# Expert mixture: weights loaded and split two experts at a time, mostly inside a written-out first unit

## The chip, the core and the metric

The program runs on one core of one Trainium2 chip. The core has TensorE (PE: matmuls into PSUM banks), VectorE (DVE), ScalarE (ACT), GpSimd (POOL) and SyncE (SP), which here only issues transfers (DMA) between the chip's memory and the on-chip SBUF. Each engine runs its own instructions in order and meets the others at semaphores. The metric is the device time of one execution in microseconds (us); lower is better.

## What is computed

The program is a graph network of two layers; the change concerns one stage of it, the feed-forward part of layer 0. Its input is the sum of two row sets in memory (`x1`, the linear-attention output, and `hidden`, the graph attention output), 6250 rows of 256. On each normalised row eight experts work, each with three 256x256 weights, and a softmax router weighs them:

```python
BN_EPS = 0.001
def _bn(h, g, b, m, v):
    return g * (h - m) * jax.lax.rsqrt(v + BN_EPS) + b
w = jax.nn.softmax(feat @ Wr + br, axis=-1)
h = jnp.einsum('bfd,edh->bfeh', x, W1) + b1
h = jax.nn.relu(_bn(h, g1, be1, m1, v1))
h = jnp.einsum('bfeh,ehk->bfek', h, W2) + b2
h = jax.nn.relu(_bn(h, g2, be2, m2, v2))
y = jnp.einsum('bfeh,ehd->bfed', h, Wo) + bo
return jnp.einsum('bfed,fe->bfd', y, w)
```

Here E (e) is 8 experts, D and H are 256, and `x` is the sum of the rows, normalised, with a leading axis of one; the result is added to that sum.

## The kernel before

`build` runs the stages one after the other; `expert_mixture` (L3023) is one stage, inside a block of its own: none of its instructions starts before the stage ahead has ended, and the next stage starts when it is done.

**Units.** The 50 tiles of 128 rows are taken four at a time (`QUAD`): 13 units, the last of two tiles. Loaded rows lie in `x` and `h` (two slots each, both in the tile `moe_xh`). A unit adds them (`front_start`), takes the statistics of the rows (`front_statistics`), a square root on ACT (`front_root`), normalises (`front_end`, into `xn`), turns the rows with PE (`turn`) and copies them to `xt` on ACT (`turned`). The router's products (L3343, `moe_route`) need `xt`.

**Split products.** Matmuls are done in three passes on split numbers: a number is its rounded high part (type fp32r) plus the low part, and a product is high*high + high*low + low*high (`product`, L3327). So every weight, `xt` (`cut_rows`) and both hidden activations (`cut_layer`) are split: `high_part` (L3090) rounds, `low_part` (L3093) subtracts.

**Steps of a unit.** `unit` goes through steps e = 0 to 9. In step e PE does the first layer of expert e (`moe_first`), the second of expert e-1 (`moe_second`) and the third of expert e-2 (`moe_third`). ACT follows the first two with the batch norm and relu (`layer`, L3285, into `h12`, tile `moe_h`); DVE splits what ACT wrote and adds the third layer's result to `x` (`gather_expert`, L3213). In steps 2, 3 and 5 DVE also prepares the next unit's rows.

**Before the first unit.** SP loads 13 small tensors (router weights, biases and batch norm parameters, L3101), then W1 into the place of `h12` and W2 into that of `xh`, 2 MB each for all eight experts. PE turns the parameters (L3314) and DVE and ACT work out scale and shift (`gain`, `shift`) of the batch norms. DVE then rounds and splits W1 and W2, 4096 elements in each of 128 partitions at a time. Wo is loaded over W1 once W1 has been split, and the rows of the first two units over W2 once that has been split. PE waits for `s_cutw` 3, all three weights split, before its loop over six pairs of units; unit 13 is written out behind the loop.

Of the kernel before, what the change touches and what calls it, by code (L numbers as in the profile page):

```python
# [10 lines left out]
ALU = mybir.AluOpType  # L11
# [3 lines left out]
P = 128  # L15
# [3007 lines left out]
def expert_mixture(nc, io, dram, keep):  # L3023
# [11 lines left out]
    with ExitStack() as stack:  # L3035
        space = Space(nc, stack, "moe")
        sb, sem = space.sb, space.sem
        h12 = sb("h12", [P, 2, 2, HALVES, QUAD * P])
        w = [h12[:, :, :, :, :].rearrange("p j k a n -> p (j k a n)").rearrange("p (e a d) -> p e a d", e=E, a=HALVES)]
        w_high, w_low = ([sb(f"w_{n}{j}", [P, E, HALVES, D], F32R) for j in range(3)] for n in ("high", "low"))  # L3040
# [8 lines left out]
        x, h = xh[:, 0], xh[:, 1]  # L3049
        w.append(xh[:, :, :, :, :].rearrange("p j k i d -> p (j k i d)").rearrange("p (e a d) -> p e a d", e=E, a=HALVES))  # L3050
        xn = sb("xn", [P, QUAD, D])
# [15 lines left out]
        s_x, s_sent = space.sems("s_x", 2), space.sems("s_sent", 2)  # L3067
        s_wj = space.sems("s_wj", 3)
        s_and1, s_and2, s_cut1, s_cut2, s_andx, s_cutx, s_andw, s_cutw = (
            sem(n) for n in ("s_and1", "s_and2", "s_cut1", "s_cut2", "s_andx", "s_cutx", "s_andw", "s_cutw"))  # L3070
        (s_w, s_free, s_dve, s_std_in, s_std, s_xn, s_xt, s_xtc, s_l1, s_h1, s_l2, s_h2, s_l3, s_acc, s_route, s_logit, s_exp, s_gate,
# [5 lines left out]
        hidden = pair_rows(dram["hidden"])  # L3077
        w_loads = [(w[j % 2], io[f"L0_ffn_{n}"].rearrange("e (a p) n -> p e a n", p=P)) for j, n in enumerate(("W1", "W2", "Wo"))]
        loads = [(wr[:, :, :], io["L0_ffn_Wr"].rearrange("(a p) e -> p a e", p=P)), (br[:, :], rows_of(io["L0_ffn_br"])),
# [12 lines left out]
        def low_part(out, whole, high):  # L3092
            return nc.vector.tensor_tensor(out, whole, high.bitcast(F32), ALU.subtract)  # L3093

        with nc.Block() as block:

            @block.sync
            def _(sp):
                with nc.allow_non_contiguous_dma(reason="small routing weights"):
                    for to, frm in loads:  # L3100
                        sp.dma_start(to, frm).then_inc(s_w, 16)  # L3101
                for j, (to, frm) in enumerate(w_loads):
                    if j == 2:
                        sp.wait_ge(s_cutw, 1)
                    sp.dma_start(to, frm).then_inc(s_wj[j], 16)
                sp.wait_ge(s_cutw, 2)
                for s in range(2):
                    load(sp, s, slice(s * QUAD, (s + 1) * QUAD))

# [17 lines left out]
            def _(dve):  # L3127
                c = Count(dve, s_dve)

                for j in range(2):  # L3130
                    dve.wait_ge(s_par, j + 1)
                    last = nc.vector.tensor_copy(par[:, j], bank1[j][:, 0:5 * 16].rearrange("p (i e) -> p i e", i=5))
                c.done(last)
                c.done(nc.vector.memset(bn_eps[:, :], EPS))
                dve.sem_inc(s_var, 1)
                dve.wait_ge(s_root, 1)
                c.done(nc.vector.reciprocal(gain[:, :, :], shift[:, :, :]))
                c.done(nc.vector.tensor_tensor(gain[:, :, :], gain[:, :, :], par[:, :, 1, :], ALU.mult))
                c.done(nc.vector.tensor_tensor(shift[:, :, :], par[:, :, 0, :], par[:, :, 3, :], ALU.subtract))
                c.done(nc.vector.tensor_tensor(shift[:, :, :], shift[:, :, :], gain[:, :, :], ALU.mult))  # L3140
                nc.vector.tensor_tensor(shift[:, :, :], shift[:, :, :], par[:, :, 2, :], ALU.add).then_inc(s_scale, 1)
                dve.wait_ge(s_w, 16 * len(loads))

# [75 lines left out]

                def unit(n, s, m, next_loaded, size=QUAD):  # L3220

                    gates(n, s, size)
                    for e in range(E + 2):
# [16 lines left out]
                        if e == 5 and next_loaded is not None:  # L3240
                            front_end(n + 1, 1 - s)

                dve.sem_inc(s_acc, 1)
                for j in range(3):
                    dve.wait_ge(s_wj[j], 16)
                    high_part(w_high[j][:, :, :, :], w[j % 2]).then_inc(s_andw, 1)
                    dve.wait_ge(s_andw, j + 1)
                    low_part(w_low[j][:, :, :, :], w[j % 2], w_high[j][:, :, :, :]).then_inc(s_cutw, 1)
                    if j == 1:
                        front_start(0, 32)  # L3250
                        front_statistics(0)
                        front_end(1, 0)
                cut_rows(1)
                STEPS = 8
                with dve.Fori(0, N_U // 2) as r:
                    c.enter(r, 2 * STEPS)
                    for s in range(2):
                        unit(r * 2 + s + 1, s, r * (2 * E) + s * E, r * 32 + (32 if s == 0 else 64))
                c.leave(N_U // 2)
                unit(N_U, 0, (N_U - 1) * E, None, REST)  # L3260

            @block.scalar
            def _(act):
                act.wait_ge(s_var, 1)
                nc.scalar.activation(shift[:, :, :], par[:, :, 4, :], ACT.Sqrt, bias=bn_eps[:, 0:1]).then_inc(s_root, 1)
                act.wait_ge(s_scale, 1)
                act.sem_inc(s_h1, 1)
                act.sem_inc(s_h2, 1)

                def front_root(n):  # L3270
# [17 lines left out]

                def unit(n, s, m, last, size=QUAD):
                    act.wait_ge(s_logit, n)  # L3290
                    nc.scalar.activation(gate[:, s, 0:size], logit[:, 0:size, :], ACT.Exp).then_inc(s_exp, 1)
                    for e in range(E + 1):
                        if e < E:
                            layer(0, m + (e + 1), e, size)
                        if e == E and not last:
                            turned(n + 1)
                        if e >= 1:
                            layer(1, m + e, e - 1, size)
                        if e == 4 and not last:
                            front_root(n + 1)  # L3300

                front_root(1)
                turned(1)
                with act.Fori(0, N_U // 2) as r:
                    for s in range(2):
                        unit(r * 2 + s + 1, s, r * (2 * E) + s * E, False)
                unit(N_U, 0, (N_U - 1) * E, True, REST)

            @block.tensor
            def _(pe):  # L3310
                pe.wait_ge(s_w, 16 * len(loads))
                for j in range(2):
                    for i in range(5):
                        last = nc.tensor.transpose(bank1[j][:, 16 * i:16 * i + 16], par_rows[:, j, i, :], keep["ident"][0:16, 0:16])  # L3314
                    last.then_inc(s_par, 1)
                pe.wait_ge(s_scale, 1)

                def turn(n, s):
# [18 lines left out]

                def unit(n, s, m, last_unit, size=QUAD):

# [6 lines left out]
                    for e in range(E + 2):  # L3346
                        if e < E:

                            if e == 0:
                                pe.wait_ge(s_cutx, n)  # L3350
                            pe.wait_ge(s_h1, m + (e + 1))
                            wide(bank1, 0, e, (xt_high, xt_low), size).then_inc(s_l1, 1)
                        if e == 1:
# [4 lines left out]
                        if 1 <= e <= E:  # L3358
                            pe.wait_ge(s_cut1, m + e)
                            pe.wait_ge(s_h2, m + e)  # L3360
                            wide(bank2, 1, e - 1, (h1_high[:, (e - 1) % 2], h1_low[:, (e - 1) % 2]), size).then_inc(s_l2, 1)
                        if e == 2:
# [6 lines left out]
                        if e >= 2:  # L3369
                            pe.wait_ge(s_cut2, m + (e - 1))  # L3370
                            pe.wait_ge(s_acc, m + (e - 1))
                            for i in range(size):
# [6 lines left out]
                pe.wait_ge(s_cutw, 3)  # L3379
                with pe.Fori(0, N_U // 2) as r:  # L3380
                    for s in range(2):
                        unit(r * 2 + s + 1, s, r * (2 * E) + s * E, False)
                unit(N_U, 0, (N_U - 1) * E, True, REST)


# [502 lines left out]
```

## Time and profile before

| | us |
|---|---|
| median of 3 runs (7068.94 to 7074.64) | 7070.54 |
| the profiled execution, its own time | 7087.27 |
| its span, first to last instruction | 7085.5 |
| PE / DVE / ACT / POOL busy in it | 5313.8 / 4842.8 / 4142.8 / 3639.1 |

The profiled execution is 16.7 us above the median; 1.8 us of its own time lie outside the span. Times within the trace are us from the span's start. The expert mixture stage lies from about 4270 to 5301, a seventh of the span. Since the stages follow one another, a stage's time is that of its own longest chain, and the busy shares of the whole span say little about it.

### The profile page before, as it was taken

The numbers are of one execution on the slowest core, as the hardware profiler recorded it, in microseconds if no ns is written. First come the engines' busy times: TensorE is split into PE (matmuls) and PEld (weight loads), VectorE is DVE, ScalarE is ACT, GpSimd is POOL, SyncE is SP. The second block draws the span as 40 slices with busy tenths as digits, with TensorE's granted clock in tenths as the row PEclk, the third lists the DMA queues.
The fourth block names the chain that finished last, engine by engine and source line by source line (L and its number), as shares of the span: only waits on it lengthen the run. The fifth ranks groups of instructions, "written<-read, shape, count | busy, mean of one in ns | idle before, by whom it ended". The sixth has DMA issues, their size and how long they took to land. (4 is left out here: it accounts for less than half of the span.)

```text
span 7085.5 us, 94548 instructions
## 1 busy us (share of the span) xinstructions
PE 5313.8 (75%) x22314; PEld 3799.3 (54%) x22314; DVE 4842.8 (68%) x13222; ACT 4142.8 (58%) x13411; POOL 3639.1 (51%) x3571
## 2 busy tenths in 40 slices
PE   1768888745888886668888616999989787877688
PEld 1645555333555554545555315888874566655346
DVE  5656666694777777767777596666662677778673
ACT  4578888874898988579889762333336322111132
POOL 3477777737777773577777700000000577777201
PEclk8878888876999998779999767999999898887789
DMA  6444444344444443444444332000007534333302
GB/s 184 124 123 116 117 118 117 106 132 139 119 121 122 121 118 104 131 138 124 118 122 118 109 108 65 19 18 27 19 23 267 166 116 128 109 107 101 105 17 74
DMA packets 484001, 763.77 MB, mean 108 GB/s; under 512 B 85543, under 2 KB 360695, under 8 KB 483511
## 3 DMA queue, kind: packets, MB, share of 16 engines
q0 software_dynamic: 166320, 446.82, 22.7%
q1 hardware_dynamic: 317335, 313.36, 13.9%
q14 instruction: 253, 2.07, 0.1%
q8 instruction: 93, 1.52, 0.1%
HBM read 622.82 MB, written 146.27 MB: 109 GB/s over the span
## 5 line engine op out<-in xcount | busy, mean ns | idle before, releaser
L1806 POOL DMA_INDIRECT gm_got<-scratch_feat,keep_src_tab x2490 | 2500.6, 1004 | 776.0 <-issue 669.6
L2028 ACT ACTIVATE gm_got<-gm_got 128x64 f32<-128x64 f32 x9828 | 2393.6, 335 | 5.8 <-DVE gm_got L1941 5.8
L2083 PE MATMUL gm_bank<-gm_got,gm_onehot 128*128 128x264 f32 x4980 | 1783.1, 466 | 385.9 <-DVE gat_acc L1966 229.4
L2083 PEld LDWEIGHTS gm_bank<-gm_got,gm_onehot 128*128 128x128 f32 x4980 | 938.4, 217 | 897.8 <-DVE gat_acc L1966 370.1
L1966 DVE TENSOR_TENSOR gat_acc<-gat_acc,gm_bank 128x264 f32 x2490 | 1059.1, 425 | 498.8 <-PE gm_bank L2083 231.5
L1114 POOL DMA_INDIRECT mix1a_got<-scratch_rel_feat,layer_rel_tab x240 | 240.4, 1002 | 1529.2 <-issue 1528.0
L1114 POOL DMA_INDIRECT mix1b_got<-scratch_rel_feat,layer_rel_tab x590 | 586.9, 995 | 190.5 <-issue 187.2
L1171 PE MATMUL mix1b_m_bank<-mix1b_got,mix1b_onehot 128*128 128x256 f32 x1180 | 379.6, 459 | 153.6 <-DVE layer_acc L1145 132.1
L837 POOL DMA_INDIRECT scratch_first<-gat_scores,keep_first_pos x150 | 216.5, 1444 | 466.9 <-DVE gat_scores L820 425.7
L1973 DVE TENSOR_TENSOR gm_onehot<-keep_iota_row,keep_dst_tab 128x896 f32<-128x896 f32 x357 | 386.5, 1083 | 25.8 <-PE gm_bank L2083 21.9
L1171 PEld LDWEIGHTS mix1b_m_bank<-mix1b_got,mix1b_onehot 128*128 128x128 f32 x1180 | 245.7, 225 | 253.3 <-DVE mix1b_onehot L1123 166.4
L3285 ACT ACTIVATE moe_h<-moe_first,moe_shift,moe_gain 128x512 f32<-128x512 f32 (+1 forms) x208 | 147.1, 759 | 350.0 <-PE moe_first L3327 350.0
L3327 PE MATMUL moe_third<-moe_w_high,moe_cuts 128*128 128x256 f32 x1600 | 315.5, 290 | 29.5 <-DVE moe_xh L3213 29.5
L1145 DVE TENSOR_TENSOR layer_acc<-layer_acc,mix1b_m_bank 128x256 f32 x590 | 242.8, 412 | 86.3 <-PE mix1b_m_bank L1171 71.9
L3327 PEld LDWEIGHTS moe_third<-moe_w_high,moe_cuts 128*128 128x128 f32 x1600 | 262.7, 196 | 38.5 <-issue 34.8
L3090 DVE CAST moe_cuts<-moe_h 128x1024 fp32r<-128x1024 f32 (+1 forms) x208 | 140.1, 674 | 198.6 <-ACT moe_h L3285 196.7
L3093 DVE TENSOR_TENSOR moe_cuts<-moe_h,moe_cuts 128x1024 fp32r<-128x1024 f32 (+1 forms) x208 | 246.4, 1185 | 7.1
L3327 PE MATMUL moe_second<-moe_cuts,moe_w_high 128*128 128x512 f32 (+1 forms) x832 | 249.9, 383 | 0.0
L3767 POOL TENSOR_TENSOR slo_x<-slo_x,slo_b_out 128x512 f32<-128x512 f32 x25 | 31.0, 1269 | 419.3 <-DMA slo_x<-scratch_x 419.3
L3285 ACT ACTIVATE moe_h<-moe_second,moe_shift,moe_gain 128x512 f32<-128x512 f32 (+1 forms) x208 | 147.3, 759 | 166.4 <-PE moe_second L3327 166.4
L1665 PE MATMUL gm_side<-gm_w,gm_fft 128*128 128x256 f32 x800 | 244.0, 387 | 0.0
L505 ACT ACTIVATE mix1b_ln_std<-mix1b_ln_mv,keep_eps 128x2 f32<-128x2 f32 x75 | 16.8, 286 | 381.2 <-DVE mix1b_ln_mv L500 381.2
(558 smaller groups left out, 10760.2 us busy)
## 6 DMA issues: line engine op xcount, KB each, us to landing
scratch_rel_feat<-rel_out SPq DMA_DIRECT2D x50, 1024.0 KB, 6.3
gm_got<-scratch_feat,keep_src_tab POOLq DMA_INDIRECT x2490, 2.8
gm_flags<-scratch_flags SPq DMA_DIRECT2D x90, 280.0 KB
gf_feat<-scratch_feat SPq DMA_DIRECT2D x75, 256.0 KB, 4.4
gf_old<-scratch_hidden SPq DMA_DIRECT2D x75, 256.0 KB, 4.7
scratch_hidden<-gf_h SPq DMA_DIRECT2D x75, 256.0 KB, 4.0
scratch_feat<-gf_row SPq DMA_DIRECT2D x50, 260.0 KB, 3.3
gm_x<-scratch_x SPq DMA_DIRECT2D x50, 256.0 KB, 3.1
```

The lines of the kernel that those rows point to most:

```text
L1114: nc.gpsimd.indirect_dma_start(out=self.got[:, u, :], out_offset=None, in_=self.table, in_offset=bass.IndirectOffsetOnAxis(ap=self.keep["r ...
L1145: nc.vector.tensor_tensor(rows, rows, self.bank[p % self.BANKS][:, i * D:(i + 1) * D], ALU.add).then_inc(self.s_acc, 1)
L1171: last = self.nc.tensor.matmul(self.bank[p % self.BANKS][:, i * D:(i + 1) * D], self.onehot[:, u, :], self.got[:, u, :], start=True, stop= ...
L1665: nc.tensor.matmul(out, self.fft[:, c, i * P:(i + 1) * P], self.w2[:, c, :], start=(c == 0), stop=False)
L1806: nc.gpsimd.indirect_dma_start(out=got[:, place // GROUPS, place % GROUPS * GROUP + j, 0:GAT_ROW], out_offset=None, in_=dram["feat"][layer ...
L1966: nc.vector.tensor_tensor(a, a, bank[j % BANKS][:, 0:GAT_SUM], ALU.add).then_inc(s_acc, 1)
L1973: nc.vector.tensor_tensor(onehot[:, half:half + GROUP, :], keep["iota_row"][:, :].unsqueeze(1).to_broadcast([P, GROUP, P]), keep["dst_tab" ...
L2028: last = nc.scalar.activation(rows, rows, ACT.Copy, scale=got[:, b, i, D + h:D + h + 1])
L2083: nc.tensor.matmul(bank[i % BANKS][:, 0:GAT_SUM], onehot[:, i % HOTS, :], got[:, v[1] % B, i, :], start=True, stop=True).then_inc(s_sum, 1)
L3093: return nc.vector.tensor_tensor(out, whole, high.bitcast(F32), ALU.subtract)
L3285: last = nc.scalar.activation((h1, h2)[j][:, e % 2, a, 0:size * P], (bank1, bank2)[j][a][:, 0:size * P], ACT.Relu, bias=shift[:, j, q:q + ...
L3327: last = nc.tensor.matmul(out, lhs(k)[i], rhs(k)[j], start=(p == 0), stop=(p == len(passes) - 1))
```

## The change

The weights are loaded and split in four groups of two experts (`AT_ONCE = 2`, 512 KB for each weight) rather than all eight at once. High parts of weights are made by ACT, low parts by DVE. Only group 0 is done ahead of the first unit. That unit is written out before the loop, and groups 1 to 3 are done within it: group g of W1 after step 2g-2, of W2 and Wo after step 2g-1 (`group_due`). The whole weights pass through places not yet used: parts of `h12` for group 0, row slot 1 for W2 and Wo of group 1, and a new tile `spare` of two places in turn for the rest. The rows of the first unit are loaded ahead of everything, those of the second once group 1 of W2 and Wo has been split. The parameters are worked out after the first unit's rows. The loop runs over five pairs of units, starting with unit 2; unit 12 is written out behind it, then unit 13 as before.

```diff
             def _(sp):
+                load(sp, 0, slice(0, QUAD))
+                for j in range(3):
+                    load_weight(j, 0)
                 with nc.allow_non_contiguous_dma(reason="small routing weights"):
                     for to, frm in loads:
                         sp.dma_start(to, frm).then_inc(s_w, 16)
-                for j, (to, frm) in enumerate(w_loads):
-                    if j == 2:
-                        sp.wait_ge(s_cutw, 1)
-                    sp.dma_start(to, frm).then_inc(s_wj[j], 16)
-                sp.wait_ge(s_cutw, 2)
-                for s in range(2):
-                    load(sp, s, slice(s * QUAD, (s + 1) * QUAD))
+                for j in range(3):
+                    load_weight(j, 1)
+                load_weight(0, 2)
+                load_weight(1, 2)
+                for j in (1, 2):
+                    sp.wait_ge(s_cutw[j], 2)
+                load(sp, 1, slice(QUAD, 2 * QUAD))
+                load_weight(2, 2)
+                for j in range(3):
+                    load_weight(j, 3)
...
+                def load_weight(j, g):
+                    if (j, g) in SPARE[2:]:
+                        before_j, before_g = SPARE[SPARE.index((j, g)) - 2]
+                        sp.wait_ge(s_cutw[before_j], before_g + 1)
+                    sp.dma_start(whole(j, g), weights[j][:, experts(g), :, :]).then_inc(s_wg[j][g], 16)
...
+                def cut_weights(j, g):
+
+                    dve.wait_ge(s_high[j], g + 1)
+                    low_part(w_low[j][:, experts(g), :, :], whole(j, g), w_high[j][:, experts(g), :, :]).then_inc(s_cutw[j], 1)
...
+                def high_weights(j, g):
+                    act.wait_ge(s_wg[j][g], 16)
+                    nc.scalar.copy(w_high[j][:, experts(g), :, :], whole(j, g)).then_inc(s_high[j], 1)
...
+        def group_due(e):
+
+            if e % 2 == 0:
+                return [(0, e // AT_ONCE + 1)] if e // AT_ONCE + 1 < W_GROUPS else []
+            return [(j, (e + 1) // AT_ONCE) for j in (1, 2)] if (e + 1) // AT_ONCE < W_GROUPS else []
```

On PE the first unit's passes wait for their group: `s_cutw[0]`, `[1]` and `[2]` at e // 2 + 1 of the expert in hand. PE now turns the first rows, then the parameters, and waits for scale and shift (`s_scale`) before the router's products.

Ahead of the first unit, DVE's order before (tiles: `moe_par`, `moe_gain`, `moe_shift` are the parameters, `moe_h` and `moe_xh` the weights in their loading places, `moe_xn` the normalised rows):

```order
L3132 COPY moe_par<-moe_first 128x80 x2
...
L3141 TENSOR_TENSOR moe_shift<-moe_shift,moe_par 128x32
L3090 CAST moe_w_high<-moe_h 128x4096
L3093 TENSOR_TENSOR moe_w_low<-moe_h,moe_w_high 128x4096
L3090 CAST moe_w_high<-moe_xh 128x4096
L3093 TENSOR_TENSOR moe_w_low<-moe_xh,moe_w_high 128x4096
L3147 TENSOR_TENSOR moe_xh<-moe_xh 128x1024
...
L3164 TENSOR_SCALAR moe_xn<-moe_xh,moe_mv,moe_std 128x256 x4
L3090 CAST moe_w_high<-moe_h 128x4096
L3093 TENSOR_TENSOR moe_w_low<-moe_h,moe_w_high 128x4096
L3090 CAST moe_xt_high<-moe_xt 128x1024
L3093 TENSOR_TENSOR moe_xt_low<-moe_xt,moe_xt_high 128x1024
```

Here the parameters stand first and the rows between the second weight and the third. DVE's order of the change at the same place (router work, `moe_logit`, begins the unit):

```order
L3189 TENSOR_TENSOR moe_xh<-moe_xh 128x1024
...
L3206 TENSOR_SCALAR moe_xn<-moe_xh,moe_mv,moe_std 128x256 x4
L3096 TENSOR_TENSOR moe_w_low<-moe_h,moe_w_high 128x1024
L3093 CAST moe_xt_high<-moe_xt 128x1024
L3096 TENSOR_TENSOR moe_xt_low<-moe_xt,moe_xt_high 128x1024
L3169 COPY moe_par<-moe_first 128x80 x2
...
L3178 TENSOR_TENSOR moe_shift<-moe_shift,moe_par 128x32
L3096 TENSOR_TENSOR moe_w_low<-moe_h,moe_w_high 128x1024 x2
L3229 TENSOR_TENSOR moe_logit<-moe_route,moe_br 128x32
```

Three roundings and three subtractions of 4096 elements have become three subtractions of 1024, the rows stand first and the parameters behind them.

Within the first unit, DVE's order of the change in steps 2 and 3 (the `moe_w_low` rows are added; the rest stood in the loop's body in the same order):

```order
L3255 SCALAR_TENSOR_TENSOR moe_xh<-moe_third,moe_gate,moe_xh 128x256 x4
L3189 TENSOR_TENSOR moe_xh<-moe_xh 128x1024
L3096 TENSOR_TENSOR moe_w_low<-moe_spare,moe_w_high 128x1024
L3093 CAST moe_cuts<-moe_h 128x1024
L3096 TENSOR_TENSOR moe_cuts<-moe_h,moe_cuts 128x1024
L3093 CAST moe_cuts<-moe_h 128x1024
L3096 TENSOR_TENSOR moe_cuts<-moe_h,moe_cuts 128x1024
L3255 SCALAR_TENSOR_TENSOR moe_xh<-moe_third,moe_gate,moe_xh 128x256 x4
L3194 BN_STATS moe_stats<-moe_xh 128x6 x4
L3198 BN_AGGR moe_mv<-moe_stats 128x2 x4
L3096 TENSOR_TENSOR moe_w_low<-moe_spare,moe_w_high 128x1024 x2
L3093 CAST moe_cuts<-moe_h 128x1024
```

A subtraction now stands behind the next unit's first sum in step 2, and two behind its statistics in step 3. On ACT the roundings stand at the end of the same steps:

```order
L3332 ACTIVATE moe_h<-moe_second,moe_shift,moe_gain 128x512 x2
L3315 CAST moe_w_high<-moe_spare 128x1024
L3332 ACTIVATE moe_h<-moe_first,moe_shift,moe_gain 128x512 x2
L3332 ACTIVATE moe_h<-moe_second,moe_shift,moe_gain 128x512 x2
L3315 CAST moe_w_high<-moe_spare 128x1024 x2
```

In the loop's body of before, ACT has only the two `moe_h` rows in each step; the one rounding (step 2) and the two (step 3) stand between them.

## Rows read from the trace of the kernel before

**Rows 1.** Timeline, SP and PE: start us, us, engine, line, (idle before <-releaser).

```profile
4270.39 0.38 SPq L3101 DMA_DIRECT2D moe_wr<-in_L_ffn_Wr  x1
...
4276.09 0.41 SPq L3101 DMA_DIRECT2D moe_par_rows<-in_L_ffn_v  x1
...
4277.01 2.00 SPq L3105 DMA_DIRECT2D moe_xh<-in_L_ffn_W  x1
4277.71 1.24 PE L3314 MATMUL moe_first<-keep_ident,moe_par_rows 16*128 16x16 f32 x10 [162.10 <-DMA moe_par_rows<-in_L_ffn_v]
```

**Rows 2.** Timeline, the parameters on DVE, first and last.

```profile
4278.45 0.24 DVE L3132 COPY moe_par<-moe_first 128x80 f32<-128x80 f32 x1 [11.49 <-PE moe_first L3314]
...
4280.86 0.19 DVE L3141 TENSOR_TENSOR moe_shift<-moe_shift,moe_par 128x32 f32<-128x32 f32 x1
```

**Rows 3.** Timeline, weights and rows ahead of the first unit.

```profile
4284.82 2.29 DVE L3090 CAST moe_w_high<-moe_h 128x4096 fp32r<-128x4096 f32 x1 [3.77 <-DMA moe_h<-in_L_ffn_W]
4287.15 4.43 DVE L3093 TENSOR_TENSOR moe_w_low<-moe_h,moe_w_high 128x4096 fp32r<-128x4096 f32 x1
...
4298.26 0.37 SPq L3085 DMA_DIRECT2D moe_xh<-scratch_x  x1
...
4303.83 1.23 DVE L3147 TENSOR_TENSOR moe_xh<-moe_xh 128x1024 f32<-128x1024 f32 x1 [5.60 <-DMA moe_xh<-scratch_hidden]
```

**Rows 4.** Timeline, from normalised rows to PE's first product.

```profile
4307.60 1.38 DVE L3164 TENSOR_SCALAR moe_xn<-moe_xh,moe_mv,moe_std 128x256 f32<-128x256 f32 x4
...
4309.13 1.09 PE L538 MATMUL moe_turn<-keep_ident,moe_xn 128*128 128x128 f32 x4 [30.18 <-DVE moe_xn L3164]
...
4311.59 0.59 ACT L3277 COPY moe_xt<-moe_route 128x512 f32<-128x512 f32 x1
...
4315.56 0.69 DVE L3090 CAST moe_xt_high<-moe_xt 128x1024 fp32r<-128x1024 f32 x1
...
4315.89 3.57 PE L3343 MATMUL moe_route<-moe_wr,moe_xt 128*128 128x8 f32 x16 [4.82 <-DVE moe_w_low L3093]
...
4319.31 0.77 PE L3327 MATMUL moe_first<-moe_xt_high,moe_w_high 128*128 128x512 f32 x1
```

**Rows 5.** Groups of ACT by form: a copy of 1024 elements.

```profile
L3775 ACT COPY slo_lhs<-ffn_slice_t 128x1024 f32 x25 | 25.7, 1045 | 63.4 <-PE slo_bank L3786 53.9 <-PEq L3779 9.5
```

**Rows 6.** DVE line L3093 alone: min/median/max ns of one, at 1024 elements.

```profile
L3093 DVE TENSOR_TENSOR moe_xt_low<-moe_xt,moe_xt_high x13: 1225/1226/1227, 4316.3 to 5246.1; 128x1024 fp32r<-128x1024 f32 x13
```

**Rows 7.** Timeline of unit 1, steps 3 and 4, PE, ACT and DVE.

```profile
4345.26 0.62 PE L3327 MATMUL moe_second<-moe_cuts,moe_w_high 128*128 128x512 f32 x2
...
4345.46 1.45 ACT L3285 ACTIVATE moe_h<-moe_first,moe_shift,moe_gain 128x512 f32<-128x512 f32 x2 [6.29 <-PE moe_first L3327]
...
4346.94 0.70 DVE L3090 CAST moe_cuts<-moe_h 128x1024 fp32r<-128x1024 f32 x1 [1.10 <-ACT moe_h L3285]
...
4351.53 1.65 DVE L3213 SCALAR_TENSOR_TENSOR moe_xh<-moe_third,moe_gate,moe_xh 128x256 f32<-128x256 f32 x4
...
4353.22 1.40 DVE L3152 BATCH_NORM_STATS2 moe_stats<-moe_xh 128x6 f32<-128x256 f32 x4
...
4353.60 0.62 PE L3327 MATMUL moe_second<-moe_cuts,moe_w_high 128*128 128x512 f32 x2
...
4355.28 0.69 DVE L3090 CAST moe_cuts<-moe_h 128x1024 fp32r<-128x1024 f32 x1
...
4356.32 0.28 PE L3327 MATMUL moe_third<-moe_w_high,moe_cuts 128*128 128x256 f32 x1
```

**Rows 8.** Windows: length; PE, PEld, DVE, ACT, POOL busy; PEclk, DMA, GB/s.

```profile
4280.00:4290.00 10.00, 0.00 (x0) 0.00 (x0) 6.06 (x7) 0.00 (x0) 0.00 (x0) 0.50 1.08 350
```

**Rows 9.** Timeline, PE's router products behind the loop's turns.

```profile
4474.75 1.95 PE L3343 MATMUL moe_route<-moe_wr,moe_xt 128*128 128x8 f32 x16 [0.71 <-issue]
...
4941.83 3.58 PE L3343 MATMUL moe_route<-moe_wr,moe_xt 128*128 128x8 f32 x16 [2.52 <-issue]
```

**Rows 10.** DMA issues of the stage: KB each, us to landing.

```profile
moe_xh<-scratch_hidden SPq DMA_DIRECT2D x10, 512.0 KB, 5.0
```

More of the change, by code:

```diff
@@ L3241, in unit @@
                             front_end(n + 1, 1 - s)
+                        if cutting:
+                            for j, g in group_due(e):
+                                cut_weights(j, g)
                 dve.sem_inc(s_acc, 1)
[L3244 to L3252, printed above, removed]
+                front_start(0, 32)
+                front_statistics(0)
+                front_end(1, 0)
+                cut_weights(0, 0)
                 cut_rows(1)
+                parameters()
+                for j in (1, 2):
+                    cut_weights(j, 0)
                 STEPS = 8
-                with dve.Fori(0, N_U // 2) as r:
+                unit(1, 0, 0, 32, cutting=True)
+                with dve.Fori(0, N_U // 2 - 1) as r:
                     c.enter(r, 2 * STEPS)
-                    for s in range(2):
-                        unit(r * 2 + s + 1, s, r * (2 * E) + s * E, r * 32 + (32 if s == 0 else 64))
-                c.leave(N_U // 2)
+                    for s in (1, 0):
+                        k = 2 - s
+                        unit(r * 2 + k + 1, s, r * (2 * E) + k * E, r * 32 + 64)
+                c.leave(N_U // 2 - 1)
+                unit(N_U - 1, 1, (N_U - 2) * E, 32 * (N_U // 2 + 1))
                 unit(N_U, 0, (N_U - 1) * E, None, REST)
@@ L3287, in layer, with unit @@
                     last.then_inc((s_h1, s_h2)[j], 1)
-                def unit(n, s, m, last, size=QUAD):
+                def unit(n, s, m, last, size=QUAD, cutting=False):
                     act.wait_ge(s_logit, n)
@@ L3297, in unit @@
                         if e >= 1:
+                            if cutting and e == 2:
+                                act.wait_ge(s_cutw[2], 1)
                             layer(1, m + e, e - 1, size)
@@ L3378, in _ @@
                 turn(1, 0)
[L3379 to L3382, printed above, removed]
+                pe.wait_ge(s_w, 16 * len(loads))
+                for j in range(2):
+                    for i in range(5):
+                        last = nc.tensor.transpose(bank1[j][:, 16 * i:16 * i + 16], par_rows[:, j, i, :], keep["ident"][0:16, 0:16])
+                    last.then_inc(s_par, 1)
+                pe.wait_ge(s_scale, 1)
+                unit(1, 0, 0, False, cutting=True)
+                with pe.Fori(0, N_U // 2 - 1) as r:
+                    for s in (1, 0):
+                        k = 2 - s
+                        unit(r * 2 + k + 1, s, r * (2 * E) + k * E, False)
+                unit(N_U - 1, 1, (N_U - 2) * E, False)
                 unit(N_U, 0, (N_U - 1) * E, True, REST)
```

90 lines of the change are left out of this document (57 added, 33 removed).

## Prediction

> **What bounds the kernel now.** The page comes first: no engine is busy for more than three quarters of the span, and the stages follow one another, so the question is what the chain of this one stage is. The timeline of its start answers it. SP issues the first small load at 4270.39, PE has the parameters at 4277.71 [rows 1], and then DVE alone works: each weight costs it 2.29 us of rounding and 4.43 us of subtraction [rows 3], 6.7 us, or 20.2 us for the three, with a wait of 3.77 us for W1 ahead of them. The rows of unit 1 can be loaded only when W2's place is free, so SP issues them at 4298.26 [rows 3]. The wait that ends last ahead of the unit is PE's for `moe_w_low`, at 4315.89; its first layer product starts at 4319.31, 48.92 us after the stage's first load [rows 4]. Behind that, in unit 1 as in the others, PE is the bound: one step takes 8.34 us (4345.26 to 4353.60, the same pass of the next expert) and PE has no gap in it [rows 7], while DVE has holes of about a microsecond. So what the stage takes ahead of 4319.31 counts in full, and work on ACT and DVE in unit 1 counts only where it makes PE wait.
>
> **The new chain ahead of unit 1, step by step.** All from 4270.39, where the rows' load now stands.
> (a) From issue to DVE's sum of the two row sets: 4298.26 to 4303.83 [rows 3], 5.57 us, to 4275.96.
> (b) Sum, statistics, square root and normalising: 4303.83 to the end of `moe_xn`, 4308.98 [rows 3, 4], 5.15 us, to 4281.11.
> (c) PE's turn and ACT's two copies: 4308.98 to 4312.18 [rows 4], 3.20 us, to 4284.31.
> (d) Splitting `xt`: 4315.56 to the end of the subtraction, 0.69 us and 1.23 us with 0.03 us between them [rows 4, 6], 1.95 us, to 4286.26.
> (e) The parameters, now behind that: 4278.45 to 4281.05 [rows 2], 2.60 us, to 4288.86.
> (f) The router's products: 4315.89 to 4319.31 [rows 4], 3.42 us, to 4292.28.
> The first product starts at 4292.28 rather than at 4319.31: 27.03 us earlier.
>
> What is taken to cost nothing, and what hides it. The three weight loads of group 0 stand behind the rows. At 350 GB/s, the rate of the stretch in which the 2 MB loads run [rows 8], 512 KB take 1.5 us, so they land at 4277.5, 4279.0 and 4280.5. ACT rounds 1024 elements in about 1.05 us, by a copy of that width [rows 5]: W1 to 4278.5, before its square root is wanted (4279.2), W2 and Wo behind its `xt` copies, 4284.3 to 4286.4, before the parameters' square root (about 4287). DVE's subtraction of W1 (1.23 us [rows 6]) fills its wait for the turn. Those of W2 and Wo, 2.45 us from 4288.86, end at 4291.3, within the router's products. The 13 small loads are issued from 4272.8 to about 4278.5, 0.48 us apart (twelve distances from 4270.39 to 4276.09) and, with 1.6 us from the last issue to use [rows 1], are there at 4280.5 to 4281; PE turns them after 4283.2, 1.24 us [rows 1], while DVE still splits. PE comes out of its long wait at a granted clock of 0.50, 1.2 GHz [rows 8]; (c) and (f) are read behind that wait, and in the changed kernel they again follow one, so I change nothing for the clock.
>
> Here a rule of the Trainium skill speaks against the change. The trace first: the thirteen small loads of [rows 1] overlap, and the last lands 1.6 us behind its issue; so DMAs in one queue do not pay their latency one after another. The page "DMA: Bandwidth & Descriptors" (section Bandwidth) says to batch transfers to 1 MiB or more, since each costs some 2.0 us fixed plus its bytes at 436 GB/s. Paid in series, five loads of 512 KB would by that page take 16 us and the 13 small ones another 26, the stage would start no earlier than now, and the change would be worth nothing.
>
> **Unit 1 with the rest of the weights.** It holds nine roundings of 1.05 us on ACT (9.4 us) and nine subtractions of 1.23 us on DVE (11.0 us) [rows 5, 6]. ACT has two activations of 1.45 us [rows 7] in a step of 8.34 us and has room. DVE is the one to count. The fullest place is behind step 3's statistics: DVE runs without a wait from its addition at 4351.53 over the statistics at 4353.22 to its next rounding at 4355.28 [rows 7], and two subtractions more, 2.45 us, move that to 4357.73. It enters step 3 hardly late, since the one subtraction of step 2 (1.23 us) falls into a hole of 1.10 us [rows 7] and what is left is absorbed by the next. From 4357.73 it has two splits (1.95 us each) and the addition (1.65 us) to do: 4363.28. PE wants the addition for its third layer at 4356.32 + 8.34 = 4364.66 [rows 7]. The margin is 1.4 us; the split itself is wanted at 4353.60 + 8.34 = 4361.94 and is there at 4359.7. Steps 4 and 5 have as much. Bounds: nothing if the margin holds; if it fails, at most the subtractions that stand beyond one per step, three of 1.23 us, 3.7 us. Below nothing it can't go, as no work leaves unit 1. I take 0.5 us, near the row.
>
> **Loads inside unit 1.** SP now holds the second unit's rows until `s_cutw[1]` and `[2]` are 2, DVE's end of step 1, some 19 us behind the first product; queued behind this wait are one 512 KB load of Wo and three of group 3. The rows land 5.6 us later by (a), 5.0 by the loads inside the stage [rows 10], and DVE wants them at the end of step 2, more than 6 us later. Each other late load has a whole step of 8.34 us against 5.0 [rows 10]. I take nothing.
>
> **The written-out unit.** PE's router products wait for "issue" 0.71 and 2.52 us behind turns of the loop [rows 9] (a third wait there is shorter). The change trades one turn for the loop's entry between units 1 and 2. Between -2.5 and 2.5 us; I take 0, since the number of crossings stays six.
>
> **Sum.** 27.0 - 0.5 = 26.5 us. Against its own time the profiled execution would be 7087.27 - 26.5 = 7060.8. The median of the runs shown lies 16.7 us below that execution; the stage's chain is the same in both, so the median becomes 7070.54 - 26.5 = 7044.0.
>
> **Rivals.**
> 1. DVE becomes unit 1's bound. For it: the 1.4 us margin is made of many small rows. Against it: holes in every step. With the 3.7 us above and a late entry into the loop, 2.5 us, it gives 7049.7.
> 2. Code loading. For it: "issue" waits of up to 2.52 us exist [rows 9], and PE gets some 600 rows of straight code. Against it: those waits stand at turns of the loop, where the code jumps, and the written-out unit has no jump. Three waits of 2.52 us give 7.6 us, 7051.6. (The Trainium skill, "Advanced Engine Details and Errata", section Sequencer Memory, ISA Cache, has instructions cached in 16 KB lines of 256 instructions, which would mean a refill from memory every so many rows of the unit; by that rule the three waits are its price if none is hidden, and no row shows code loading as such.)
> 3. The parameters come late, so the change does not do what it says. If each small load took its 1.6 us of landing alone behind the bulk (4280.5), the last would be there at 4301.6; with PE's 1.24, (e) and (f) the first product starts at 4308.9, 10.4 us earlier than now: 7060.1, within 0.2%. Against it: [rows 1] shows them overlap.
> 4. Unit 1 becomes one chain, rounding, subtraction, the release of the place in `spare`, the next load: nothing hides. Nine of 2.28 us are 20.5 us, five loads that wait for a subtraction at 5.0 us are 25, together 45.5, against 27.0 gained: 18.5 us slower, 7089.0. It decides from the point where 27 of the 45.5 us are exposed. Against it: the order allots every group a step of 8.34 us ahead of its use, and 2.28 + 5.0 us fit in.
>
> **How the numbers follow.** Forecast (24 to 29 us gained) 0.74; rival 1, 0.09; rival 2, 0.09; rival 3, 0.05; rival 4, 0.03. The range leaves out rivals 3 and 4 and reaches from 7036 (a turn of the loop's 2.5 us gained, and some 5 us by which later stages or runs may differ) to 7055. A measurement of this kernel can tell 0.2%, 14.1 us, from no change; faster than that are the forecast and rivals 1 and 2, 0.92; within it rival 3, 0.05; slower rival 4, 0.03.
>
> **What would show it.** In the changed kernel's trace: PE's first `moe_first` product by the weights about 21.9 us after the stage's first load (now 48.92); the parameters' matmuls behind the turn, with no wait for a DMA; in unit 1 no new wait of PE above 1.4 us, and none of ACT for a weight load; the first two routers' products as far apart as now or some 1 us less. It is wrong if ACT or PE waits for DMA at the start (rival 3), if DVE's additions end behind PE's want in steps 3 to 5 (rival 1), or if PE shows "issue" waits inside unit 1 (rival 2).

## The result, and the profile after

The change makes the kernel faster: 7051.09 us (median of 9 runs, 7041.63 to 7057.47) against 7074.64 us for the kernel before (9 runs, 7068.94 to 7081.69). The ratio is 0.9963, 95% interval 0.9953 to 0.9972, which is 20 to 33 us; the medians stand 23.6 us apart. Forecast were 7044.0 us, 26.5 us below the 7070.54 us of the three runs then known.

The profiled execution of the changed kernel took 7042.02 us, 45.3 us less than the profiled one of before. Not all of that is the change's: the stage begins at 4256.02 rather than 4270.39 [rows 1], and nothing ahead of it was touched. These 14.4 us are what two executions may differ by. So the two traces are compared from the stage's first load on. After, the timeline of the way to the first product (start us, us, engine, line, idle before it and its releaser):

```profile
4256.02 0.38 SPq L3088 DMA_DIRECT2D moe_xh<-scratch_x  x1
...
4259.27 1.74 SPq L3134 DMA_DIRECT2D moe_wr<-in_L_ffn_Wr  x1
...
4262.36 1.23 DVE L3189 TENSOR_TENSOR moe_xh<-moe_xh 128x1024 f32<-128x1024 f32 x1 [9.78 <-DMA moe_xh<-scratch_hidden]
...
4263.86 1.04 ACT L3315 CAST moe_w_high<-moe_h 128x1024 fp32r<-128x1024 f32 x1 [14.47 <-DMA moe_h<-in_L_ffn_W]
...
4266.13 1.38 DVE L3206 TENSOR_SCALAR moe_xn<-moe_xh,moe_mv,moe_std 128x256 f32<-128x256 f32 x4
...
4266.49 0.42 SPq L3134 DMA_DIRECT2D moe_par_rows<-in_L_ffn_v  x1
...
4270.05 0.59 ACT L3324 COPY moe_xt<-moe_route 128x512 f32<-128x512 f32 x1
4270.12 1.25 PE L3442 MATMUL moe_first<-keep_ident,moe_par_rows 16*128 16x16 f32 x10 [0.59 <-DMA moe_par_rows<-in_L_ffn_v]
...
4274.57 0.19 DVE L3178 TENSOR_TENSOR moe_shift<-moe_shift,moe_par 128x32 f32<-128x32 f32 x1
4274.68 2.35 DVE L3096 TENSOR_TENSOR moe_w_low<-moe_h,moe_w_high 128x1024 fp32r<-128x1024 f32 x2
4274.81 3.58 PE L3397 MATMUL moe_route<-moe_wr,moe_xt 128*128 128x8 f32 x16 [3.44 <-DVE moe_shift L3178]
...
4278.25 0.77 PE L3381 MATMUL moe_first<-moe_xt_high,moe_w_high 128*128 128x512 f32 x1
```

The first product stands 22.23 us behind the first load, against 48.92 [rows 1, 4]: 26.69 us are gone. DVE's weights ahead of the unit are down to three subtractions of 1.2 us, two of them within PE's router products. Here and below, "first product" and "unit 2" are the starts of PE's first `moe_first` pass and of unit 2's router products, counted from the stage's first load; "last" is the start of unit 13's router products.

| kernel | first product | unit 2 | unit 1 takes | last | units 2 to 12 |
|---|---|---|---|---|---|
| before | 48.92 | 125.74 | 80.2 | 985.65 | 859.9 |
| after | 22.23 | 98.65 | 79.9 | 955.21 | 856.6 |

Unit 1 (router products to router products, 4274.81 to 4354.67) is not longer for the nine roundings and nine subtractions in it. Units 2 to 12, in which the change alters nothing but the place of the loop's turns, differ by 3.4 us; the experiments show what that is.

Inside unit 1 the fullest place is step 3, as for [rows 7]. After, on DVE and PE:

```profile
4310.11 1.65 DVE L3255 SCALAR_TENSOR_TENSOR moe_xh<-moe_third,moe_gate,moe_xh 128x256 f32<-128x256 f32 x4
4311.80 1.41 DVE L3194 BATCH_NORM_STATS2 moe_stats<-moe_xh 128x6 f32<-128x256 f32 x4
...
4313.65 2.33 DVE L3096 TENSOR_TENSOR moe_w_low<-moe_spare,moe_w_high 128x1024 fp32r<-128x1024 f32 x2
4315.90 0.69 DVE L3093 CAST moe_cuts<-moe_h 128x1024 fp32r<-128x1024 f32 x1
...
4319.62 1.65 DVE L3255 SCALAR_TENSOR_TENSOR moe_xh<-moe_third,moe_gate,moe_xh 128x256 f32<-128x256 f32 x4
...
4323.24 0.28 PE L3381 MATMUL moe_third<-moe_w_high,moe_cuts 128*128 128x256 f32 x1
```

DVE works from 4310.11 to 4321.27 without a wait, and PE wants its last addition at 4323.24: a margin of 2.0 us. The waits of PE from the first product to 5230, within unit 13 (who waited for whom: us in total, times, longest), name no weight and no load:

```profile
PE moe_third L3381 <- DVE moe_xh L3255: 25.5, 11, 2.3
PE moe_first L3381 <- ACT moe_h L3332: 19.8, 13, 1.5
PE moe_third L3381 <- issue: 2.3, 1, 2.3
PE moe_route L3397 <- issue: 2.1, 2, 1.9
```

The first is the wait at each full unit's end, which the kernel before has too; the third is unit 1's own one at the same place, of the same 2.3 us. The profile names no releaser for it, but DVE's addition ends at 4351.61 and PE goes on at 4351.72, so it is the same wait.

### The profile page after: what moved, and what is told of

Its sections match the earlier page's. It is cut to its first block and busy times, and to the rows that moved or that the text cites. A ratio compares the mean times of both kernels' runs of the same rounds, so it can differ in the third digit from the quotient of the medians.

```text
span 7040.2 us, 94521 instructions
## 1 busy us (share of the span) xinstructions
PE 5305.9 (75%) x22314; PEld 3792.5 (54%) x22314; DVE 4835.2 (69%) x13228; ACT 4152.7 (59%) x13423; POOL 3635.4 (52%) x3571
## 3 DMA queue, kind: packets, MB, share of 16 engines
q0 software_dynamic: 166320, 446.82, 23.3%
q1 hardware_dynamic: 317479, 313.36, 14.1%
## 5 line engine op out<-in xcount | busy, mean ns | idle before, releaser
L3093 DVE CAST moe_cuts<-moe_h 128x1024 fp32r<-128x1024 f32 (+1 forms) x208 | 140.1, 673 | 187.1 <-ACT moe_h L3332 185.4
```

## Experiments

Some of the runs fell on two chips on which the kernel before takes 8005 and 8022 us rather than 7071 to 7076. The steps of the stage take the same time on all of them, so its rows are compared across all runs, and times of whole kernels only as ratios to the kernel before on the same chip. All kernels but one are edits of the changed one.

**The two kernels again.** Unaltered, on one chip.

> The kernel before, unaltered, for a trace on the same chip. Expected of the stage: the first product 48.9 us and unit 2's router products 125.7 us behind the stage's first load, within 1 us of the first trace, so that the stages can be compared across chips.

> The changed kernel itself, unaltered, beside the others of this call on the same chip. Expected of the stage: the first product 22.2 us and unit 2's router products 98.7 us behind the stage's first load, within 1 us of the first trace, wherever the stage starts; of the time: 0.993 to 0.998 of the kernel before.

Before: first product 48.97, unit 2 at 125.78, last 978.34; the profiled execution took 7071.03 us. The change: 22.54, 102.27 and 958.73; 7052.49 us median of 11 runs against 7075.79 of 17, ratio 0.9964 (0.9952 to 0.9977). The first products are as before. Unit 2 misses what I expected by 3.6 us: unit 1 took 83.2 us rather than 79.9. PE has no wait in it that the first trace lacks; its granted clock is what differs. Windows of 8 us in steps 2 and 3 of this run (length; busy time of PE, PEld, DVE, ACT, POOL with counts; granted clock, DMA share, GB/s):

```profile
4300.00:4308.00 8.00, 8.00 (x36) 6.31 (x35) 7.32 (x8) 6.23 (x9) 0.00 (x0) 1.00 0.23 73
4308.00:4316.00 8.00, 8.00 (x41) 7.16 (x40) 6.95 (x11) 1.18 (x2) 0.00 (x0) 0.79 0.40 125
4316.00:4324.00 8.00, 8.00 (x48) 7.11 (x47) 6.79 (x11) 4.44 (x7) 0.00 (x0) 1.00 0.19 66
```

PE is busy throughout, yet gets 41 matmuls through at a mean clock of 0.79; the same stretch of the first trace (4298.50 to 4306.50) has 48 at 1.00. PE's passes fall behind the first trace by 1.8 us there, and by another 1.5 us at the unit's end, behind the wait of 2.3 us that PE has there in every full unit:

```profile
4360.00:4364.00 4.00, 1.73 (x15) 1.55 (x14) 3.19 (x6) 0.97 (x1) 0.00 (x0) 1.00 0.00 0
4364.00:4368.00 4.00, 4.00 (x24) 4.00 (x23) 0.00 (x0) 0.00 (x0) 0.00 (x0) 0.57 0.00 0
```

In the first trace of the change no such fall follows that wait in unit 1. Such dips come in every trace, at other units each time: over thirteen traces the time of a full unit other than the first is between 76.3 and 81.0 us, and units 2 to 12 together between 851.4 and 862.6. No run shows what sets them off. So the 3.4 us of the first pair need no cause in the change, and the second pair, whose stages differ by 19.6 us in all rather than by 30.4, had its dips the other way round.

**Taking the work out of unit 1 again.** All groups are rounded and subtracted ahead of unit 1.

```diff
                 for j in (1, 2):
                     cut_weights(j, 0)
+                for g in range(1, W_GROUPS):
+                    for j in range(3):
+                        cut_weights(j, g)
...
-                        if cutting:
-                            for j, g in group_due(e):
-                                cut_weights(j, g)
```

ACT's `high_weights` are moved likewise.

> Edit: the changed kernel, but groups 1 to 3 of the weights are rounded and subtracted ahead of unit 1 rather than within it; all else is as in the change. My theory (the work inside unit 1 is hidden, so the gain lies in taking it there): ahead of the unit DVE has nine subtractions of 1.2 us, 11 us, and the late loads wait for a place in the spare tile, some 6 to 10 us more; the gates stand behind them, so the distance from the stage's first load to unit 2's router products grows from 98.7 us to 112 to 120 us, and the time is 13 to 21 us above the changed kernel's 7051, near 7065 to 7072. Rival (the work costs PE as much inside unit 1 as ahead of it, and the gain is only that of the rows' early load): at most 6 us more than the changed kernel, below 7057.

Unit 2 comes at 118.67, 20.0 us later than in the changed kernel, and the whole gain is gone: 8000.98 us median of 10 runs, ratio 0.9997 (0.9979 to 1.0015). The first product itself is where it was (22.38); the wait is behind it. Waits from there on:

```profile
PE moe_first L3381 <- ACT moe_h L3332: 17.2, 1, 17.2
DVE moe_w_low L3096 <- ACT moe_w_high L3315: 10.4, 5, 4.7
ACT moe_w_high L3315 <- DMA moe_spare<-in_L_ffn_W: 7.6, 3, 4.0
...
ACT moe_w_high L3315 <- DMA moe_spare<-in_L_ffn_Wo: 5.4, 2, 4.8
```

PE waits 17.2 us for the first activation, which on ACT stands behind all roundings and behind an exponential that needs DVE's router work; that in turn stands behind all subtractions. DVE has 11 us of subtractions there and waits 10.4 us for roundings, because ACT waits 13.0 us in all for five loads into `spare`, each of which can start only when a subtraction has freed its place; PE's router products and first passes cover only the beginning of this. Inside unit 1 the same loads are covered. After the wait PE's granted clock is 0.50 once more (4854.05 to 4858.05). The rival, by which the work would cost as much in unit 1 as ahead of it, is refuted.

**The order of the loads.** SP issues group 0 and the 13 small loads ahead of the rows.

```diff
-                load(sp, 0, slice(0, QUAD))
                 for j in range(3):
                     load_weight(j, 0)
...
+                load(sp, 0, slice(0, QUAD))
```

> Edit: the changed kernel, but SP issues group 0 of the weights and the 13 small loads ahead of the rows of unit 1. My theory (the chain to PE's first product begins with the rows' load): the rows are issued 7 to 10 us later and the first product moves by as much, from 22.2 us behind the stage's first load to 29 to 33 us. Rival (the parameters' arrival, 14.1 us behind the first load in the changed kernel, bounds as well): the parameters come some 3 us earlier and the first product moves by less than 5 us.

The first product moves to 29.89, 7.7 us later, and unit 2 by 8.1 to 106.78. The rows' load heads the chain; the parameters do not. From the rows' issue to DVE's sum it takes 5.59 us here.

**How much DVE could bear.** Each of the nine subtractions is done twice.

```diff
+                                dve.wait_ge(s_high[j], g + 1)
+                                c.done(low_part(w_low[j][:, experts(g), :, :], whole(j, g), w_high[j][:, experts(g), :, :]))
                                 cut_weights(j, g)
```

> Edit: the changed kernel, but each of the nine subtractions inside unit 1 is done twice, 11 us more of DVE work in steps 0 to 5. My theory (DVE has a margin of about 1.4 us in steps 3 and 5 and holes of a microsecond elsewhere): PE now waits for DVE, and unit 1, from its router products to those of unit 2, grows from 79.9 us to 84 to 90 us. Rival (DVE is so far from PE's path that even this is hidden): below 81 us. Rival (DVE already bounds unit 1 in the changed kernel): all 11 us show, 91 us.

Unit 1 takes 89.4 us, within the 84 to 90 expected. PE now does wait for DVE, in two places for a split activation and once for a weight:

```profile
PE moe_second L3383 <- DVE moe_cuts L3096: 4.3, 2, 2.5
...
PE moe_first L3383 <- DVE moe_w_low L3096: 0.5, 1, 0.5
```

Not all of the 9.5 us is DVE's. Pass by pass PE is 6.4 us behind the change after its last such wait (step 7). Another 1.7 us come right behind it at a granted clock of 0.50 (4892.6 to 4895.9), and 1.5 us in a second dip behind the wait at the unit's end (4909.7 to 4913.0). In step 5 the addition is late as well as the split activation: PE waits 2.5 us for the split at its second layer and 0.46 us more at its third, which starts at 4876.38, 0.10 us after DVE's addition ends. The profile puts that wait down to "issue".

**Roundings on DVE as well.** Inside unit 1 DVE makes the high parts too, 6.2 us more.

```diff
+                                dve.wait_ge(s_wg[j][g], 16)
+                                high_part(w_high[j][:, experts(g), :, :], whole(j, g)).then_inc(s_high[j], 1)
                                 cut_weights(j, g)
```

> Edit: the changed kernel, but inside unit 1 DVE makes the high parts of the weights too (nine roundings of 0.69 us, 6.2 us more on DVE), and ACT none. My theory (DVE's additions in steps 3 and 5 end 1.3 to 1.7 us before PE wants them, as worked out in the prediction): the two roundings of step 3 add 1.4 us, just the margin, so PE waits for at most 2 us in all and unit 1 takes 79.9 to 82 us. Rival (the margin is smaller than worked out, and the 9.5 us that the doubled subtractions cost came in proportion to the work): 5 us and more, 85 us.

Unit 1 takes 82.9 us, 1 us above what I expected. Pass by pass PE falls behind by 0.9 us at step 5 and 0.4 us at step 7, 1.6 us at the last third layer, as forecast; the other 1.5 us come after it, in a stretch of 4 us at a granted clock of 0.57 (first product 22.87, unit 2 at 102.33, last 960.70).

```profile
PE moe_third L3380 <- issue: 2.7, 2, 2.3
...
PE moe_second L3380 <- DVE moe_cuts L3096: 0.3, 1, 0.3
```

One of the two waits in the first row is that of 0.47 us at step 5. PE goes on there at 4883.14, and DVE's addition, the one behind step 3's statistics, has ended at 4883.04. So the addition is what is late first, as the prediction had it. Behind the first product it ends 2.8 us later than in the change and not 1.4: the rounding of step 2 does not fit into a hole. So the margin is real but not wide: rounding on ACT rather than on DVE is worth 1.6 us.

**What else stands ahead of unit 1.** PE waits for scale and shift ahead of the router's products, which do not need them. Here it waits only for the copies out of its bank, behind those products.

```diff
-                pe.wait_ge(s_scale, 1)
                 unit(1, 0, 0, False, cutting=True)
...
                                 pe.wait_ge(s_cutx, n)
+                                if cutting:
+                                    pe.wait_ge(s_var, 1)
```

DVE's subtractions of W2 and Wo of group 0 are moved behind the gates.

> Edit: the changed kernel, but PE waits for the parameters' copies out of its bank (s_var) behind the router's products of unit 1 and no longer for scale and shift ahead of them, and DVE does the subtractions of W2 and Wo of group 0 behind the gates. My theory (the router's products of 3.4 us stand behind the parameters for no need): the first product starts 17 to 19 us behind the stage's first load rather than 22.2, and unit 2's router products come 3 to 4.5 us earlier than 98.7 us. Rival (ACT's scale, shift and exponential bound the first activation instead): the first product is earlier, but the first activation and unit 2 are not by more than 1 us. In the time of the whole kernel this can hardly be seen: 7047 against 7051.

First product 18.78, unit 2 at 95.25, both 3.4 us earlier than in the change, as the theory has it. The time is 7983.46 us, ratio 0.9960 (0.9940 to 0.9981).

**The small loads on another queue.** ACT issues them, and the parameters are worked out first.

```diff
+                    for to, frm in loads:
+                        act.dma_start(to, frm).then_inc(s_w, 16)
```

> Edit: the changed kernel with the 13 small loads issued by ACT's queue instead of SP's, the parameters worked out ahead of the splitting of the first rows, the turn of the first rows behind the parameters' turn on PE, and the router's products not waiting for scale and shift. My theory (the small loads bind in the variant with the early router's products, as their last lands 14.1 us behind the first load): the first product starts 16.5 to 18 us behind the stage's first load, against 18.8 in that variant, and unit 2's router products 93 to 95 us behind it. Rival (the small loads are held back by the 2.5 MB ahead of them in the DMA engines, whichever queue issues them): they still land at about 14 us and, now standing ahead of the turn, move the first product to 20 us or later.

The rival holds, and 16.5 to 18 us for the first product are missed. Issue is done by 8.6 us, but the last lands 14.1 us behind the first load, just as from SP's queue, and the rows come later:

```profile
4262.71 0.38 SPq L3088 DMA_DIRECT2D moe_xh<-scratch_x  x1
...
4270.76 1.23 DVE L3186 TENSOR_TENSOR moe_xh<-moe_xh 128x1024 f32<-128x1024 f32 x1 [11.48 <-DMA moe_xh<-scratch_hidden]
4270.90 0.45 ACTq L3310 DMA_DIRECT2D moe_par_rows<-in_L_ffn_v  x1
...
4276.80 1.25 PE L3444 MATMUL moe_first<-keep_ident,moe_par_rows 16*128 16x16 f32 x10 [168.75 <-DMA moe_par_rows<-in_L_ffn_v]
```

8.05 us from the rows' issue to DVE, against 6.34 in the change and 6.20 to 6.98 in the other runs with its order of loads. First product 21.84, unit 2 at 98.29, last 951.82; 7041.54 us in one run.

**Keeping PE's clock up.** The same with 56 transposes at PE's start, whose results nobody reads.

```diff
+                for i in range(56):
+                    nc.tensor.transpose(bank3[i % 2][:, 0:P], keep["ident"][:, :], keep["ident"][:, :])
```

> Edit: as the variant with the small loads on ACT's queue, and PE does 56 transposes of the identity into an unused bank at the stage's start, while it waits for its first rows; they are extra work whose result nobody reads. My theory (PE comes out of its long wait at a granted clock of 0.5 and does the router's products and the first expert's first layer at that clock, some 3.5 and 4.9 us that take 1.9 and 2.7 at full clock): unit 1 becomes 2 to 4 us shorter, so that unit 2's router products come 2 to 4 us earlier than in that variant. Rival (the first unit waits for ACT and DVE, not for PE, there): less than 1 us. Rival (the transposes come in the way of the first rows' turn): the first product is later than in that variant.

First product 22.11, unit 2 at 98.07: nothing gained, and the theory's size is missed. The windows tell why:

```profile
4262.00:4266.00 4.00, 4.00 (x37) 3.89 (x35) 0.36 (x1) 0.00 (x0) 0.00 (x0) 0.98 0.82 268
4266.00:4270.00 4.00, 0.12 (x2) 0.00 (x0) 3.42 (x12) 1.34 (x2) 0.00 (x0) 0.87 1.11 330
4270.00:4274.00 4.00, 2.05 (x14) 2.02 (x15) 1.33 (x6) 0.31 (x1) 0.00 (x0) 0.50 1.08 335
```

The granted clock rose to 1.00 while PE was busy and was back at 0.50 after PE had been idle for 5.8 us ahead of the parameters. The time is 7043.56 us, ratio 0.9960 (0.9944 to 0.9976).

With 80 of them, on the variant with the early router's products:

> Edit: the variant with the early router's products (small loads on SP, as in the change), and 80 transposes of the identity into an unused bank on PE at the stage's start, extra work whose result nobody reads, enough to last up to the first rows' turn. My theory (in the run with 56 of them the clock had risen and fell back while PE was idle ahead of the turn): PE now does the turn, the router's products and the first layer at full clock, the router's products take 1.9 us rather than 3.5 and the twelve first-layer passes 2.9 rather than 4.9, and unit 2's router products come 2.5 to 4 us earlier than in the variant without them, at 91 to 93 us behind the first load. Rival (the gaps of 1 to 2 us that remain are enough to lose it): no change, 95 us.

The turn itself ran at full clock (`moe_turn` 0.66 us rather than 1.11 us), but PE then stood idle 1.41 us for the parameters, and within the router's products the granted clock fell to 0.50 (0.88 over 4834.38 to 4836.38, 0.50 over the 6 us behind it). First product 17.54, unit 2 at 94.39, last 953.93. Of 2.5 to 4 us expected 0.9 came.

At last the small loads between rows and group 0 as well, and ACT's square root ahead of its first rounding:

> Edit: as the variant with 80 transposes, and SP issues the 13 small loads between the rows and the weights of group 0, and ACT does the rows' square root ahead of the first weight's rounding. My theory (the parameters' arrival is what PE's router products wait for): the parameters come at 8 to 10 us rather than 14.1 behind the first load, the first product starts at 16 to 17.5 us, and unit 2's router products 90 to 92.5 us behind it; the kernel takes 0.995 to 0.997 of the time before, 5 to 8 us less than the change, which is at the edge of what can be told. Rival (the first weight's load, now 6 us later, takes the parameters' place): the first product is not earlier than in the variant with 80 transposes.

First product 16.56, the earliest of all and within the expected 16 to 17.5, but unit 2 at 95.09 misses the expected 90 to 92.5 (last 953.57). The granted clock was back at 0.50 by the end of the router's products, although PE's waits from the turn on had been of 0.28 and 0.45 us only (ahead of the turn and of these products); and unit 1 ended in a dip (0.57 over 4908 to 4912). 7989.31 us, ratio 0.9962 (0.9945 to 0.9979). It takes 5.7 us off the way to the first product and yet does no measurably better than the change: the three variants timed lie at 0.9960 to 0.9962, the change at 0.9963 and 0.9964. Of the 5.7 us, 5.0 are left at ACT's first activation (22.07 against 27.08), since PE's first twelve passes all ran at 0.50 here and the last of them at 1.00 in the change, and 3.6 us at unit 2, the rest being the dip. PE's wait for that activation is 1.54 us in this run as in the change. A gain of 4 us in the stage is less than the intervals of these ratios can tell.

## Why the prediction was right

**The bound and the sum.** PE's first product did stand behind DVE's weights, and the chain put in their place runs in the order given. Its terms:

| step | predicted | measured |
|---|---|---|
| (a) rows, issue to sum | 5.57 | 6.34 |
| (b) to normalised rows | 5.15 | 5.15 |
| (c) turn and copies | 3.20 | 3.13 |
| (d) splitting `xt` | 1.95 | 2.00 |
| (e) parameters | 2.60 | 2.17 |
| (f) router's products | 3.42 | 3.44 |
| sum, with the hand-overs | 21.89 | 22.23 |

Only (a) and (e) are off. (a) was 0.77 us too small; in the six other runs with this order of loads it is 6.20 to 6.98. Why is open: it is not the number of loads queued behind the rows, for with group 0 and the small loads ahead of them and four weight loads issued right behind they took 5.59 us, and with only the small loads close behind them 6.59. In (e) the wait for PE's second set of parameters fell out.

**What was taken to cost nothing.** The roundings and subtractions hid where they were said to. Mis-sized were the small loads: forecast at 10.1 to 10.6 us, used at 14.1 us. SP's issue of them took from 4259.27 to 4266.91 and not 6.1 us, and the last was used 3.6 us after its issue rather than the 1.6 us of [rows 1]. They did wait behind the bulk, but that is not all: the DMA engines moved 268 GB/s over 4264.02 to 4266.02 and 23 GB/s over the next 2 us, so the 2.5 MB had gone through when the last one was issued at 4266.49. What its own 3.6 us are is open. PE waited 0.59 us for that, hidden since (e) came later. The variant with early router's products shows where this error would have mattered: there PE's wait of 0.46 us for them lies on the path.

**Unit 1.** I took 0.5 us and it is nothing that can be seen (79.9 against 80.2 us). The margin, worked out at 1.4 us, is 2.0 us, and the place of it is right: with DVE's roundings added, PE is late first at step 5, by the addition behind step 3's statistics.

**Loads inside unit 1 and the written-out unit.** ACT waited for late loads by at most 0.9 us, off PE's path. PE shows no wait where unit 1 gives way to the loop; its router products wait for "issue" twice, 2.1 us in all, against 3.9 us in three before.

**The sum against the time.** 26.7 us in the way to the first product, by the traces; 23.6 and 23.3 us by the medians of two comparisons, a little under the 24 to 29 us of the forecast, with intervals that hold 26.5. The median lies 7.1 us above 7044.0; 4.1 us of that are the kernel before itself, whose median over nine runs is 7074.64 and not the 7070.54 from which I counted, and the rest is within the interval. The time alone would not have decided for the forecast: 7051.09 is nearer to rival 1's 7049.7 and rival 2's 7051.6 than to 7044.0. What decides is the stage's trace.

**The rivals.** Rival 1 (DVE bounds unit 1) was refuted by the trace, and shown to begin where DVE gets 6 us more. Rival 2 (code loading): no "issue" wait in unit 1 but the old one at its end, which is DVE's addition, and that over 843 instructions of PE (421 matmuls and 422 weight loads) rather than some 600. Here the Trainium skill, "Advanced Engine Details and Errata", section ISA Cache, has cache lines of 256 instructions, which would mean several refills in the written-out unit; if they happen, this trace shows none on PE's path. Rival 3 (parameters late) was right in that they came late, in part behind the bulk, and wrong in size, 3.6 us and not 21. The page "DMA: Bandwidth & Descriptors" of the Trainium skill gives the 2.0 us and 436 GB/s, in its section "Anatomy of one DMA — SWDGE (gpsimd) path", as a fit for transfers issued by GpSimd. Paid one after another that fixed cost would have eaten the gain. The trace does not show it between loads that lie in SP's queue: the first weight was ready 1.5 us behind the rows (4262.36, 4263.86), which is 512 KB at 350 GB/s. Rival 4 (one chain) is what the first experiment built outside the unit: there it cost 20.0 us.

## What to carry to other kernels

Preparing constants ahead of a loop can be cut into groups and spread over a written-out first iteration; it is then free as long as the engine that does it keeps its place in the busiest step, and that is to be counted step by step, not by its share of busy time. Of the 27 us gained here the hiding was worth 20 and the loads' order 8 (each measured alone, so they need not add up). Where a stage differs by tens of us and executions of the whole by as much, count from the stage's own first instruction.

## What the runs showed of the hardware

- Thirteen loads of 4 to 8 KB were used 14.1 us behind the stage's first load, both from SP's queue behind 2.5 MB and from ACT's queue beside it, and 7.3 us behind it where they stood alone. From ACT's queue they delayed the rows on SP's to 8.05 us, from 6.20 to 6.98 us.
- PE's granted clock dips below 1.00 in the midst of dense work, 0.79 over 8 us with 41 matmuls in place of 48, at changing places, costing a unit up to some 3 us of 78.
- Raising PE's granted clock early with work that nobody reads did not last. After 56 transposes it was 1.00, and 0.50 for the parameters' turn after 5.8 us idle. After 80 it was 1.00 through the rows' turn and fell to 0.50 in the router's products, behind a wait of 1.41 us in one run and behind waits of 0.28 and 0.45 us in another.
- A wait that the profile puts down to "issue" can be one for another engine: 0.47 us at PE's third layer, 0.10 us behind the end of DVE's addition.
